# Layer 1 of a two-layer AdaLN model: extra work beside the attention tiles placed anew, and part of VectorE's work given to GpSimd

## The chip, the core and the metric

The kernel runs on one core of a Trainium2 chip, in one launch. The metric is the device time in microseconds. TensorE multiplies matrices and transposes, VectorE and ScalarE read and write both SBUF and PSUM, GpSimd works on SBUF alone and issues the indirect DMAs, and SyncE issues nearly all other DMAs. Each engine runs its own instructions strictly in the order in which they are written, and they wait for one another on semaphores. So an instruction that waits holds up everything behind it on its engine.

## The reference

Eight sequences of 512 tokens with 128 channels go through two layers; each adds a gated attention branch and then a gated feed-forward branch to `x`:

```python
h = _layernorm(x) * (1 + ca) + sa
x = x + ga * attention(h)
h = _layernorm(x) * (1 + cb) + sb
x = x + gb * feed_forward(h)
```

In layer 0 the attention is a Nystrom one with an iterated inverse, and the feed-forward is a top-1 mixture of experts with a capacity. In layer 1 the attention has 16 heads of 8 channels, a bias that depends on the distance of query and key, and a gate, `a * sigmoid(g)`. Its feed-forward is a whole block of its own:

```python
x = x + _mla(_rmsnorm(x, g1), Wq, Wdkv, Wuk, Wuv, Wo)      # 16 causal heads
x = x + _moe(_rmsnorm(x, g2), gate_w, w1, w2)              # top 2 of 8 experts
```

## The kernel before

**Two phases.** Layer 0 takes the first 650 us or so and is not touched. Layer 1 (`layer1_phase`) is one software pipeline of 713 steps. Two attentions run through it, tile by tile. A tile is 128 queries of one head against up to 512 keys; a batch (one sequence) has 64 tiles, so each attention has 512 tiles. Attention `a=0`, the one with the bias, takes tile `m` in step `m`. Attention `a=1`, the causal one, follows `LATE = 136` steps later. So steps 0 to 135 hold one attention, 136 to 511 both (the mixed steps), and 512 to 647 the second alone. I call 64 steps a block: block `s` is steps `64s` to `64s+63`, and `i` is the step within it.

**What one step does.** For `a=0`: TensorE forms the scores, VectorE adds the bias strip and takes the row maximum (`shift`, L2601, into `l_XY`), GpSimd forms maximum minus score (`L2053`), TensorE transposes the tile three steps after the shift (L2350), ScalarE takes the exponential out of PSUM (L2162), and TensorE multiplies by the values for four tiles at a time (L2384). For `a=1`: scores, VectorE's masked maximum, a second score product in turned form (L2361, with the maxima as three more rows of `l_stack`), the exponential, the values. TensorE may run at most three score tiles ahead of VectorE's shifts, since `ps` banks 0 to 2 hold them.

**The extras.** Everything else is written into these steps by hand, by tables of step numbers:

- `pre(b)`: the layer-0 experts' output is gathered (`gather`, L2042, four indirect DMAs), scaled (L2662), added to `x` (L2668), normalised and projected to q, k, v of `a=0`.
- `mid(b)`: the gate of attention 0 is applied (L2689, L2694), `x` updated (L2698), then a layer norm (L2632, L2710, L2713), an RMS norm and the projections for `a=1`.
- `split`: q and k are each cut into three bf16 parts. VectorE subtracts the first part (L2652) and casts the second (L2655); GpSimd forms the third (`last_part`, L2103). `store_parts` writes the parts to DRAM, and `stack_up` reads them back into `l_stack`, six DMAs for 16 tiles.
- `router(b)`: top-2 routing of batch `b`, from step `MOE_START[b]` on (44 of a block, for nearly all). `scatter` (L2077) sends tokens to DRAM with eight indirect DMAs, and `plan_blocks` (L2814 to L2861) makes, once for two batches, the table of expert blocks. Then come the block pairs of experts (L2484, L2459) and the gathers that combine them (L2092).

**What is where, before.** In a mixed block, VectorE's extras stand at i = 3, 7, 9, 11 (`pre`), 22 to 28 (splits of `a=0`), 23 to 43 (`mid`), and 49 to 55 (splits of `a=1`). The plan is at 30, 32, 34, 36 and 38 in blocks 5 and 7. GpSimd's scatters are at 18 to 32, one in two steps, and the gathers at 40, 44, 48 and 52. SyncE stores the parts of `a=1` at 57, waits there until they have landed, and loads the first stack of the next batch at 62. `CLEAR_AT` has it zero 2 MB of `rows_dram` at i = 56 of blocks 0, 2, 3, 4 and at step 130.

## Time and profile before

| | |
|---|---|
| median of 3 runs | 1846.85 us (1842.99 to 1851.0) |
| the profiled execution | 1861.73 us, its span 1860.0 us |
| mean granted TensorE clock | 0.95 |
| busy: TensorE | 1617.7 us (87%) |
| busy: VectorE | 1326.5 us (71%) |
| busy: ScalarE | 1007.1 us (54%) |
| busy: GpSimd | 779.3 us (42%) |

The profiled execution took 0.8% more than the median of the runs. Its shares of busy time are means over stages with different limits, so they do not say what bounds a stage. TensorE's matmuls are pipelined and their ends are modelled: a TensorE shown as 100% busy need not be at its peak, but idle time shown there is idle. Windows below are in us from the span's start. Step 0 of layer 1 starts at about 693 us (the first shift on VectorE), step 136 at 849 us, step 512 at about 1571 us, and the last tile of `a=1` is shifted at 1816 us.

### The profile page before, as it was taken

To read this page: it belongs to the slowest core of one execution; us is meant where nothing else is said; L and a number is where in the kernel's file an instruction comes from. 1 tells how busy PE (TensorE), PEld (TensorE's weight loads), DVE (VectorE), ACT (ScalarE), POOL (GpSimd) and SP (SyncE) were. 2 spreads that over 40 slices of the span, in tenths; PEclk is the share of its full clock that TensorE was granted. 3 is DMA by queue.
4 is the path that set the end of the run, shared out by engine and by line. 5 is a ranking of instruction groups with operands and counts; after the bars stand their busy time and mean duration, and the time that the engine had idled before them with its cause. 6 is when DMAs were issued, how large, how long until landed. Compare 5 with 4: busy or idle time off the path is not lost.

```text
span 1860.0 us, 50554 instructions
## 1 busy us (share of the span) xinstructions
PE 1617.7 (87%) x19264; PEld 1179.7 (63%) x19264; DVE 1326.5 (71%) x4176; ACT 1007.1 (54%) x2196; POOL 779.3 (42%) x1021
## 2 busy tenths in 40 slices
PE   3899898899883939989999999989999988888887
PEld 2677676777772727766666666656767766544545
DVE  6678777876761127788778798897886786685646
ACT  1545454455451316665666667666666656564532
POOL 3111311220115237786656566565464574243210
PEclk7899999999995969999999999999999999988999
DMA  3631122122004424344423325143452333535321
GB/s 111 190 94 46 40 84 65 36 69 82 5 7 122 157 81 155 131 151 151 160 64 128 125 84 164 56 147 98 131 161 88 114 127 111 161 98 162 109 62 53
DMA packets 143839, 194.53 MB, mean 105 GB/s; under 512 B 21920, under 2 KB 110176, under 8 KB 142320
## 3 DMA queue, kind: packets, MB, share of 16 engines
q1 hardware_dynamic: 129312, 171.75, 29.6%
q0 software_dynamic: 5760, 14.03, 2.4%
q10 hardware_dynamic: 8528, 5.51, 1.0%
q8 instruction: 156, 2.56, 0.6%
q14 instruction: 83, 0.68, 0.1%
HBM read 142.39 MB, written 50.69 MB: 104 GB/s over the span
## 4 chain that ended last, share of the span: by engine, by line
PE 44%; DVE 9%; issue 7%; ACT 5%; DMA 1%; POOL 1%; SPq 0%; another core or an unknown queue 0%; ACTq 0%; POOLq 0%; DVEq 0%
PE ps L2350 9%; PE ps L2333 7%; PE ps L2384 6%; PE ps L2394 3%; DVE l_XY L2601 3%; PE ps L2361 3%; ACT PT L2162 2%; PE ps L1229 2%; PE ps L2484 2%; PE ps L1238 2%; PE ps L2459 2%; PE ps L2410 2%; DVE ps L2601 1%; PE ps L2431 1%; PE ps L2522 1%
## 5 line engine op out<-in xcount | busy, mean ns | idle before, releaser
L2053 POOL TENSOR_SCALAR l_XY<-l_XY,l_nmax 128x512 f32<-128x512 f32 x512 | 374.9, 737 | 295.9 <-DVE l_nmax L2601 287.6
L2601 DVE CUSTOM_DVE_ANT_0 l_XY<-ps,strips 128x512 f32<-128x512 f32 x512 | 347.7, 687 | 170.4 <-PE ps L2333 115.2
L2162 ACT ACTIVATE PT<-ps 128x512 f32<-128x512 f32 x512 | 307.3, 601 | 248.0 <-PE ps L2350 236.3
L2333 PE MATMUL ps<-l_stack 72*128 72x512 bf16 (+3 forms) x1024 | 350.9, 348 | 50.1 <-DVE l_nmax L2601 35.5
L2350 PE MATMUL ps<-ident,l_XY 128*128 128x128 f32 x2048 | 320.6, 279 | 1.7 <-ACT PT L2162 1.4
L2350 PEld LDWEIGHTS ps<-ident,l_XY 128*128 128x128 f32 x2048 | 236.9, 142 | 91.0 <-issue 56.8
L2601 DVE CUSTOM_DVE_ANT_0 ps<-ps,mask 128x384 f32<-128x384 f32 (+3 forms) x512 | 250.2, 496 | 24.3 <-PE ps L2333 20.2
L2361 PE MATMUL ps<-l_stack 75*128 75x256 bf16 (+3 forms) x512 | 157.2, 308 | 22.0 <-ACT PT_odd L2165 7.5
L2333 PEld LDWEIGHTS ps<-l_stack 72*128 72x128 bf16 x1024 | 101.1, 99 | 100.5 <-DVE l_nmax L2601 55.7
L2384 PE MATMUL ps<-PT,v_aug 128*10 128x128 f32 x4096 | 137.6, 275 | 6.8 <-ACT l_O_sb L2171 6.4
L2165 ACT ACTIVATE PT_even<-ps 128x512 f32<-128x512 f32 (+1 forms) x256 | 125.1, 494 | 22.8 <-PE ps L2363 17.3
L2384 PEld LDWEIGHTS ps<-PT,v_aug 128*10 128x10 f32 x4096 | 100.3, 92 | 39.1 <-ACT PT L2162 12.4
L531 POOL DMA_INDIRECT slots_in<-h,slot_all x32 | 32.5, 1016 | 207.6 <-DVE slot_all L1106 200.3
L2363 PE MATMUL ps<-mask_turned,ident_b 128*128 128x128 bf16 x512 | 113.9, 223 | 0.0
L2601 DVE DVE_READ_ACCUMULATOR2_ANT l_nmax<- 128x1 f32 x1024 | 113.3, 111 | 0.0
L2165 ACT ACTIVATE PT_odd<-ps 128x384 f32<-128x384 f32 (+1 forms) x256 | 98.4, 388 | 27.4 <-PE ps L2363 15.0
L684 PE MATMUL ps<-X,AV 64*64 64x64 f32 x2560 | 92.7, 221 | 13.4 <-DVE X L1125 12.7
L684 PEld LDWEIGHTS ps<-X,AV 64*64 64x64 f32 x2560 | 81.8, 134 | 27.0 <-DVE X L1125 12.6
L684 PE MATMUL ps<-AV,Q 64*64 64x128 f32 (+1 forms) x1280 | 78.0, 275 | 23.5 <-DVE Q L1125 23.5
L2361 PEld LDWEIGHTS ps<-l_stack 75*128 75x128 bf16 x512 | 51.0, 100 | 66.1 <-issue 18.4
L684 PEld LDWEIGHTS ps<-AV,Q 64*64 64x64 f32 x1280 | 68.8, 141 | 30.3 <-DVE Q L1125 27.0
L2363 PEld LDWEIGHTS ps<-mask_turned,ident_b 128*128 128x128 bf16 x512 | 50.9, 99 | 46.9 <-issue 5.3
(372 smaller groups left out, 3215.9 us busy)
## 6 DMA issues: line engine op xcount, KB each, us to landing
l_stack<-parts_dram SPq DMA_DIRECT2D x384, 96.0 KB
...
rows_dram<-mask SPq DMA_DIRECT2D x6, 2048.0 KB, 8.9
...
```

Of the source, the lines that this page charges most:

```text
L684: last = nc.tensor.matmul(out(h), lhs(h), rhs(h), start=True, stop=True)
L1229: nc.tensor.matmul(ps[:, 2 + f, :], w1_e[:, e, f * P:(f + 1) * P], xT_e[:, e % 2], start=True, stop=True).then_inc(hidden_ready, 1)
L2053: nc.gpsimd.tensor_scalar(XY[:, c % XY_BUFS], XY[:, c % XY_BUFS], -1.0, nmax[:, c % 8:c % 8 + 1], ALU.mult, ALU.add).then_inc(y_pool, 1)
L2162: nc.scalar.activation(PT[:, u % QUADS, j], src.rearrange("p (k q) -> p k q", q=P), ACT.Exp).then_inc(moved, 1)
L2165: nc.scalar.activation(turned_keys(q)[:, j], src[:, 0:T - q * P], ACT.Exp).then_inc(moved, 1)
L2333: nc.tensor.matmul(ps[:, n % 3, 0:w], stack[0:STACK, 0, h, q * P:(q + 1) * P], stack[0:STACK, 1, h, 0:w], start=True, stop=True).then_inc( ...
L2350: last = nc.tensor.transpose(ps[:, to, k * P:(k + 1) * P], XY[:, c % XY_BUFS, k * P:(k + 1) * P], ident[:])
L2361: nc.tensor.matmul(ps[:, to, 0:T - k * P], stack[:, 1, h, k * P:(k + 1) * P], stack[:, 0, h, k * P:T], start=True, stop=False)
L2363: nc.tensor.matmul(ps[:, to, 0:P], ident_b[:], mask_turned[:], start=False, stop=True).then_inc(turned, 1)
L2384: last = nc.tensor.matmul(o[32 * j:32 * j + VW], v[:, k, 4 * head_group(0, g) + j, :], PT[:, u % QUADS, j, k, :], start=(k == 0), stop=(k ...
L2394: last = nc.tensor.matmul(ps[32 * j:32 * j + VW, o_bank(1, g), k * P:T], v_aug[1][u // 16 % 2][:, k, 4 * (g % 4) + j, :], turned_keys(k)[: ...
L2601: nc.vector.tensor_tensor_reduce(out=dst, in0=src, in1=add, scale=-1.0, scalar=3.0e38, op0=ALU.add, op1=ALU.min, accum_out=low).then_inc(s ...
```

## The change

No matrix product is added or taken away. `s` and `i` are as above.

- **split**: for all but the first batch, VectorE writes the second bf16 part straight from the subtraction, one instruction in place of two. GpSimd does the subtraction into `qk` once more (`first_less`) before `last_part`.
- **additions to x** in `pre` and `mid` go from VectorE to GpSimd (`x_added`, `x_gated`).
- **the layer norm of `mid`**: four `tensor_scalar` and two wide tensor instructions become eight `scalar_tensor_tensor` of 128 columns.
- **places**: tables `MID`, `LAST_MID`, `PRE` name the steps. The scaling of the gathered rows goes from i = 3 of a block to i = 53 and 62 of the block before. The gathers stand at 44, 47, 49, 50. The plan is in six pieces at i = 27, 29, 37, 41, 43, 46. Scatters go one in four steps, i = 17 to 45. Other extras move by a few steps.
- **SyncE**: the wait for the landed parts goes from the store to the load that needs them. The parts of `a=0` are stored at 44 and not at 30, those of `a=1` at 62 and not at 57. The first stack of a batch of `a=1` is loaded at 65 (i = 1) and not at 62; for the last batch, step 577 and not 570.

```diff
-MIXED_STAGES = dict(wo=1, add=3, square=5, ..., count=28, place=37, gates=37, scatter=38, plan=(50, 52, 54, 56, 58), fold=41)
+MIXED_STAGES = dict(wo=3, add=5, square=9, ..., count=26, place=36, gates=36, scatter=37, plan=(47, 49, 57, 61, 63, 66), fold=41)
...
-SCATTER_EVERY = {0: 2, 1: 2, 2: 2, 3: 2, 4: 4, 5: 1}
+SCATTER_EVERY = {0: 4, 1: 4, 2: 4, 3: 4, 4: 3, 5: 1}
...
-GATHER_AT = 40
+PRE_GATHERS, MID_GATES = (44, 47, 49, 50), (19, 20)
...
-    steps += [(LATE + GROUP * k - 10 - (4 if k >= 27 else 0), 1, k) for k in range(4 * B)]
+    steps += [(LATE + GROUP * k - (7 if k % 4 == 0 else 10 + (4 if k >= 27 else 0)), 1, k) for k in range(4 * B)]
...
-                    sp.wait_ge(parts_stored, 32 * n + 32)
 
                 def stack_up(a, k):
                     b = k // 4
+                    if k % 4 == 0:
+                        sp.wait_ge(parts_stored, 32 * PART_NO[a, b] + 32)
...
-                    if pre is not None and i == 30:
+                    if pre is not None and i == PRE["store"]:
                         store_parts(0, pre)
-                    if mid is not None and i == 57:
+                    if mid is not None and i == mid_of(mid)["store"]:
                         store_parts(1, mid)
...
+                def x_added(b):
+                    pool.wait_ge(y_scaled, E + b)
+                    nc.gpsimd.tensor_tensor(x_rows(b), x_rows(b), y0[:], ALU.add).then_inc(x_in, 1)
+
+                def x_gated(b):
+                    pool.wait_ge(mid_sum, E + b + 1)
+                    nc.gpsimd.tensor_tensor(x_rows(b), x_rows(b), h_of(b), ALU.add).then_inc(x_mid, 1)
+
+                def first_less(k, a, b):
+                    pool.wait_ge(second_part, 2 * PART_NO[a, b] + k + 1)
+                    order.link(nc.gpsimd.tensor_tensor(qk[:, k, :], qk[:, k, :], parts[:, k, 0, :], ALU.subtract))
...
-                        link(nc.vector.tensor_tensor(qk[:, k, :], qk[:, k, :], parts[:, k, 0, :], ALU.subtract))
+                        if PART_NO[a, b]:
+                            nc.vector.tensor_tensor(parts[:, k, 1, :], qk[:, k, :], parts[:, k, 0, :], ALU.subtract).then_inc(second_part, 1)
...
-                def pre(b, i):
-                    if i == 3:
+                def scaled(b, half_):
+                    if half_ == 0:
                         dve.wait_ge(gathered, 16 * TT * (b + 1))
...
+                    if m == pre_step(b, "y0"):
+                        scaled(b, 0)
+                    if m == pre_step(b, "y1"):
+                        scaled(b, 1).then_inc(y_scaled, 1)
...
-                    if i == 33:
-                        wait_xn(("xm", b))
-                        link(normalised(1, b))
+                    if i == mid_of(b)["norm"]:
+                        dve.wait_ge(var_ready, VARIANCES[1, b] + 1)
+                        for t in range(TT):
+                            last = nc.vector.scalar_tensor_tensor(out=h[:, t, :], in0=x_tile(b, t), scalar=mean_var[1][:, t, 0:1],
+                                                                  in1=mid_rows[:, 2], op0=ALU.subtract, op1=ALU.mult)
+                        link(last)
```

VectorE in steps 356 and 357 (block 5, i = 36 and 37), before. L2713 is the second wide instruction of the layer norm, L2842 to L2849 a piece of the plan; the shifts (`ISA`) are the tiles' own work.

```order
L2710 TENSOR_TENSOR h_tok<-l_xn,mid_rows 128x512 [waits l1_dve_order]
L2601 ISA l_XY,l_nmax<-ps,strips 128x512 [waits scores_ready,turned]
L2601 ISA l_nmax 128x1
L2601 ISA ps,l_nmax<-ps,mask 128x512 [waits scores_ready]
L2601 ISA l_nmax 128x1
L2842 TENSOR_REDUCE block_at<-l_gated 128x24 [waits l1_dve_order]
L2845 TENSOR_SCALAR plan<-expert_of 128x24
L2847 TENSOR_TENSOR block_at<-block_at,block_row 128x24 [waits l1_dve_order]
L2849 TENSOR_SCALAR plan<-block_at 128x24 [waits l1_dve_order]
L2601 ISA l_XY,l_nmax<-ps,strips 128x512 [waits scores_ready,turned]
L2601 ISA l_nmax 128x1
L2601 ISA ps,l_nmax<-ps,mask 128x512 [waits scores_ready]
```

The same two steps in the changed kernel:

```order
L2645 ISA l_nmax 128x1
L2645 ISA ps,l_nmax<-ps,mask 128x512 [waits scores_ready]
L2645 ISA l_nmax 128x1
L2645 ISA l_XY,l_nmax<-ps,strips 128x512 [waits scores_ready,turned]
L2645 ISA l_nmax 128x1
L2645 ISA ps,l_nmax<-ps,mask 128x512 [waits scores_ready]
L2645 ISA l_nmax 128x1
L2774 SCALAR_TENSOR_TENSOR h_tok<-h_tok,l_rstd,mid_rows 128x128 [waits l1_rstd_ready,l1_dve_order]
L2774 SCALAR_TENSOR_TENSOR h_tok<-h_tok,l_rstd,mid_rows 128x128 x3
L2890 SCALAR_TENSOR_TENSOR shift_of<-first_row,start_of 128x8 [waits l1_dve_order]
L2892 TENSOR_TENSOR l_gated<-block_row,start_of 128x192
L2895 TENSOR_TENSOR l_gated<-l_gated,named 128x192 [waits l1_dve_order]
```

The four instructions of the plan have left step 356, and in step 357 the narrow norm instructions stand together with an earlier piece of the plan.

SyncE where block 1 ends and block 2 begins, before. `parts_dram<-l_parts` stores the parts of the first batch of `a=1`; `x6` is its first stack, and the two rows behind it are a stack of `a=0`.

```order
L1869 DMA parts_dram<-l_parts 128x3x512 [waits l1_parts_ready] x2
L1836 DMA gb_now<-mods_dram 128x128 [waits l1_x_in,l1_parts_stored]
L1836 DMA mid_rows<-mods_dram 128x128 [waits mid_rows_used]
L1836 DMA mid_rows<-mods_dram 128x128 x2
L1883 DMA l_stack<-parts_dram 24x1x2048 x6
L1883 DMA l_stack<-parts_dram 24x1x2048 [waits scores_ready]
L1883 DMA l_stack<-parts_dram 24x1x2048 x5
```

In the changed kernel:

```order
L1855 DMA mid_rows<-mods_dram 128x128 [waits mid_rows_used]
L1855 DMA mid_rows<-mods_dram 128x128 x2
L1888 DMA parts_dram<-l_parts 128x3x512 [waits l1_parts_ready] x2
L1903 DMA l_stack<-parts_dram 24x1x2048 [waits scores_ready]
L1903 DMA l_stack<-parts_dram 24x1x2048 x5
L1903 DMA l_stack<-parts_dram 24x1x2048 [waits l1_parts_stored]
L1903 DMA l_stack<-parts_dram 24x1x2048 x5
```

The store now stands behind the rows of `mid`, the stack of `a=0` comes ahead of that of `a=1`, and the wait for the landed parts is at the latter.

SyncE shortly before tile 448 of `a=1` (its last batch), before. `l_stack<-max_rows` brings the maxima that the turned scores of an earlier stack need.

```order
L1869 DMA parts_dram<-l_parts 128x3x512 [waits l1_stacked3,l1_stacked2,l1_stacked4,l1_parts_ready]
L1869 DMA parts_dram<-l_parts 128x3x512 [waits l1_parts_ready]
L1883 DMA l_stack<-parts_dram 24x1x2048 [waits scores_ready,l1_parts_stored]
L1883 DMA l_stack<-parts_dram 24x1x2048 x5
L1915 DMA l_stack<-max_rows 3x16x128 [waits moved]
```

In the changed kernel:

```order
L1888 DMA parts_dram<-l_parts 128x3x512 [waits l1_stacked3,l1_stacked2,l1_stacked4,l1_parts_ready]
L1888 DMA parts_dram<-l_parts 128x3x512 [waits l1_parts_ready]
L1935 DMA l_stack<-max_rows 3x16x128 [waits moved]
L1903 DMA l_stack<-parts_dram 24x1x2048 [waits scores_ready,l1_parts_stored]
L1903 DMA l_stack<-parts_dram 24x1x2048 x5
```

The maxima now go ahead of the six loads of the stack, and not behind them.

## Rows read from the trace of the kernel before

**Rows 1.** Busy time by windows, steps 22 to 40 of blocks 1 to 7

```profile
1218.00:1256.00 38.00, 30.50 (x333) 21.23 (x331) 36.68 (x118) 22.92 (x56) 24.15 (x33) 1.00 0.36 118
...
1484.00:1518.00 34.00, 29.06 (x317) 20.04 (x315) 32.63 (x113) 20.37 (x52) 25.17 (x33) 0.95 0.33 111
sum 223.00, PE 198.37 PEld 140.86 DVE 211.76 ACT 141.08 POOL 150.54; mean PE 28.34 PEld 20.12 DVE 30.25 ACT 20.15 POOL 21.51
```

**Rows 2.** The same view, steps 0 to 14 of blocks 1 to 6

```profile
sum 136.00, PE 126.21 PEld 92.46 DVE 123.10 ACT 81.01 POOL 71.97; mean PE 21.03 PEld 15.41 DVE 20.52 ACT 13.50 POOL 11.99
```

**Rows 3.** The same view, steps 48 to 62 of blocks 1 to 6

```profile
sum 161.00, PE 157.44 PEld 106.34 DVE 116.58 ACT 109.75 POOL 96.13; mean PE 26.24 PEld 17.72 DVE 19.43 ACT 18.29 POOL 16.02
```

**Rows 4.** Waits, TensorE, 693 to 1571 us: total us, times, longest

```profile
PE ps L2333 <- DVE l_nmax L2601: 31.9, 52, 1.4
```

**Rows 5.** Lines of VectorE: count, busy us, mean ns, idle us before

```profile
L2632 DVE TENSOR_SCALAR l_xn<-x_sb,l_mean_var,l_rstd 128x128 f32<-128x128 f32 x60 | 23.8, 457 | 0.2 <-POOL l_rstd L2048 0.2
...
L2655 DVE CAST l_parts<-l_qk 128x512 bf16<-128x512 f32 x30 | 17.3, 578 | 0.0
...
L2662 DVE SCALAR_TENSOR_TENSOR y<-y,gate_keep,gb_now 128x128 f32<-128x128 f32 x28 | 9.6, 401 | 1.4 <-DMA gb_now<-mods_dram 1.4
...
L2698 DVE TENSOR_TENSOR x_sb<-x_sb,h_tok 128x512 f32<-128x512 f32 x8 | 7.2, 903 | 0.0
L2710 DVE TENSOR_TENSOR h_tok<-l_xn,mid_rows 128x512 f32<-128x512 f32 x8 | 7.1, 882 | 0.0
...
L2713 DVE TENSOR_TENSOR h_tok<-h_tok,mid_rows 128x512 f32<-128x512 f32 x8 | 6.3, 783 | 0.0
```

**Rows 6.** The same view, first and last of eleven in the plan

```profile
L2834 DVE TENSOR_REDUCE expert_of<-l_gated 128x24 f32<-128x192 f32 x3 | 1.0, 345 | 0.0
...
L2861 DVE CAST placed_index<-placed 128x16 int32<-128x16 f32 x3 | 0.5, 174 | 0.1
```

**Rows 7.** The same view, GpSimd

```profile
L2103 POOL TENSOR_TENSOR l_parts<-l_qk,l_parts 128x512 bf16<-128x512 f32 x30 | 34.9, 1164 | 2.4 <-DVE l_parts L2655 2.2
...
L2099 POOL TENSOR_TENSOR l_gated<-l_gated,b_gate_sb 128x512 f32<-128x512 f32 x16 | 20.7, 1293 | 9.9 <-ACT l_gated L2193 9.8
```

**Rows 8.** One line's instructions, L2698: durations in ns

```profile
L2698 DVE TENSOR_TENSOR x_sb<-x_sb,h_tok x8: 681/700/1515, 795.9 to 1621.8; 128x512 f32<-128x512 f32 x8
```

**Rows 9.** Timeline of VectorE and GpSimd in block 5: start, length

```profile
1225.25 2.15 DVE L2694 SCALAR_TENSOR_TENSOR h_tok<-h_tok,mid_rows 128x512 f32<-128x512 f32 x1
...
1225.68 1.16 POOL L2103 TENSOR_TENSOR l_parts<-l_qk,l_parts 128x512 bf16<-128x512 f32 x1
```

**Rows 10.** Timelines of the gathers' end and of SyncE; the page's DMA issues

```profile
664.05 1.01 POOL L2042 DMA_INDIRECT y<-slots_out,slot_all  x1 [0.30 <-issue]
...
666.67 1.14 DVE L2662 SCALAR_TENSOR_TENSOR y<-y,gate_keep,gb_now 128x128 f32<-128x128 f32 x4 [8.74 <-DMA y<-slots_out,slot_all]
...
748.76 0.58 SPq L1959 DMA_DIRECT2D rows_dram<-mask  x1
...
rows_dram<-mask SPq DMA_DIRECT2D x6, 2048.0 KB, 8.9
```

**Rows 11.** Timelines of SyncE and TensorE, end of block 1

```profile
829.61 5.29 SPq L1869 DMA_DIRECT2D parts_dram<-l_parts  x2
837.47 0.33 SPq L1836 DMA_DIRECT2D gb_now<-mods_dram  x1
...
839.27 8.36 SPq L1883 DMA_DIRECT2D l_stack<-parts_dram  x12
...
848.12 0.22 PE L2333 MATMUL ps<-l_stack 72*128 72x128 bf16 x1
```

**Rows 12.** Timelines of SyncE and TensorE, 1655 to 1665 us

```profile
1657.60 4.16 SPq L1883 DMA_DIRECT2D l_stack<-parts_dram  x6
1661.80 0.78 SPq L1915 DMA_DIRECT2D l_stack<-max_rows  x1
...
1664.50 0.59 PE L2361 MATMUL ps<-l_stack 75*128 75x512 bf16 x1 [2.34 <-DMA l_stack<-max_rows]
```

More of the change, by code:

```diff
@@ L2110, in _ @@
                 for m in range(STEPS):
+                    for b in range(1, B):
+                        if m == pre_step(b, "x"):
+                            x_added(b)
                     s, i = divmod(m, TILES)
@@ new lines, in first_pre @@
+                def first_pre():
+                    scaled(0, 0)
+                    link(scaled(0, 1))
+                    linked()
+                    nc.vector.tensor_tensor(x_rows(0), x_rows(0), y0[:], ALU.add).then_inc(x_in, 1)
+                    dve.wait_ge(x_in, 1)
+                    statistics(0, 0)
+                    linked()
+                    variance(0)
+                    normalised(0, 0).then_inc(tok_ready, 1)
+                    for k in range(2):
+                        for part in range(2):
+                            split(k, 0, 0, part)
@@ L2886, in router @@
                         gate_pair(b)
-                    if b == GROUPS[g][-1] and k in p["plan"]:
-                        plan_blocks(g, p["plan"].index(k))
+                    for step in range(len(p["plan"])):
+                        if b == GROUPS[g][-1] and k == p["plan"][step]:
+                            plan_blocks(g, step)
                 def block_product(n):
```

157 lines of the change are left out of this document (86 added, 71 removed).

## The prediction

> **What bounds the kernel now.** I read the busy times by window first. Up to 693 us nothing changes, so only the 1167 us behind that count. In the seven stretches of steps 22 to 40, one in each of blocks 1 to 7, VectorE is busy for 211.8 of 223 us (95%) and TensorE for 198.4, so TensorE is idle for 24.6 us [rows 1]. The two worst are those with the plan, blocks 5 and 7: idle 38.0 - 30.5 = 7.5 us and 34.0 - 29.1 = 4.9 us. In steps 0 to 14 of six blocks VectorE has 123.1 of 136 us (91%) and TensorE is idle for 9.8 us [rows 2]. In steps 48 to 62 it is the other way round: TensorE 157.4 of 161 us (98%), VectorE 116.6 (72%) [rows 3]. The waits name the cause: TensorE's scores waited 31.9 us in 52 places for VectorE to free a bank of scores [rows 4]. So VectorE bounds two stretches of each block and TensorE the rest. A microsecond taken from VectorE counts in the first two only, and only up to TensorE's idle time there.
>
> **VectorE relieved, steps 22 to 40.** For each block with both parts of the work: two casts go, 2 x 0.578 = 1.16 us; the addition to `x` goes, 0.90 us; the norm goes from 4 x 0.457 + 0.882 + 0.783 = 3.49 us to eight narrow instructions, which the trace has in one form like them at 0.401 us, 3.21 us, so 0.28 us goes [rows 5]. That is 2.3 us. Of the plan, eleven instructions leave the stretch; the first takes 0.345 us and the last 0.174 us [rows 6], at a mean between them of 0.26 us some 2.9 us. So block 5 sheds 5.2 us against 7.5 us idle; block 7, which has no casts there, sheds 0.90 + 0.28 + 2.9 = 4.1 us against 4.9 us; the other five shed 2.3 x 5 = 11.7 us against 24.6 - 12.4 = 12.2 us. Sum 21.0 us.
>
> **Steps 0 to 14.** Four scalings (4 x 0.401 us [rows 5]) and an addition of the form of L2698 (0.90 us) leave, 2.5 us in each of six blocks, 15 us, against 9.8 us idle [rows 2]: 9.8 us at most. The scalings reappear at i = 53 and 62, where VectorE has 28% to spare; that hides them [rows 3], and without that cover they would cost 1.6 us a block.
>
> **How much of the 30.8 us comes.** At most all of it, at least nothing. VectorE's remaining work is in lumps of up to eight small instructions in a step, and TensorE's lead is three score tiles. In steps 0 to 14, where VectorE is busy for 91%, TensorE still idles for 7% of the time [rows 2]; seven points of 223 us in the other stretches would be 15 us of idle that stays. I take half, **-15.5 us**.
>
> **GpSimd.** It gets two subtractions per split pair and an addition, which I price by the two-input rows at 1.16 and 1.29 us [rows 7]; two of its eight scatters leave steps 22 to 40. It was busy 150.5 of 223 us there [rows 1]: 67%. Added 2 x 1.16 + 1.29 = 3.6 us less about 2 x 1 us is 1.6 us in 32, so 72%. It negates a tile two steps before TensorE needs it, which hides lumps of up to some 3 us. At nothing, up to 3 us in block 0 where steps are short.
> What it does to VectorE is another matter. The addition L2698 took 0.68 us at least, 0.70 in the median and 1.52 at most [rows 8], and the scaling at 1225.25 us took 2.15 us while GpSimd formed a third part [rows 9]. So VectorE's work on two SBUF operands stretches beside GpSimd's. The half above contains this at about 4 us.
> The Trainium skill (GPSIMD Engine Reference, Key points) says that GpSimd shares its SBUF interfaces with VectorE and contends with VectorE instructions that have two SBUF inputs. By that rule the trace agrees. It speaks against the change, since work taken from VectorE for GpSimd comes back as longer VectorE instructions; a rival below takes it to its end.
>
> **The gather's landing, new in VectorE's queue.** The scaling of the gathered rows now stands at i = 53, three steps behind the last gather (i = 50), with VectorE's shifts queued behind it and TensorE, GpSimd and ScalarE behind those. The last of the first gathers was issued at 664.05 us and VectorE went on at 666.67 us [rows 10]: 2.6 us, on quiet queues. In block 0 a step takes about 1 us, and SyncE zeroes 2 MB from 748.76 us on, which takes 8.9 us to land [rows 10], just where the last gather would be issued (749 to 750 us). VectorE comes to the scaling at about 751 us. If the gather lands behind the zeroes, at 757 us, it waits 6 us, less about 3 us that TensorE has in hand; if it lands in 2.6 us, about 1 us. Bounds 0 and 6, I take **+3 us**. In later blocks three steps are 4.5 to 6 us: nothing, at most 2 us each.
>
> **The first stack of `a=1`, moved behind a stack of `a=0`.** Before, SyncE issued the parts by 834.9 us, had them landed at 837.47, and issued both stacks from 839.27 on, 4.2 us each; TensorE took the first score of `a=1` at 848.12 us [rows 11]. Now GpSimd makes the last part three steps later and in two instructions, about 839 us; SyncE issues the stack of `a=0` until 843.3 and that of `a=1` until 847.5 us, and the landing comes after. It took 2.6 us for the parts (834.9 to 837.47), so 850 us at the earliest and 854 us if two stacks at once slow it. The wait is 2 to 6 us, **+3.5 us**. TensorE's queue stands, and all others with it. In later blocks a step takes 1.5 to 2 us, the load is needed six steps on (9 us or more) and takes 4.2 + 4.2 us of issuing plus the landing, from a store that is itself three steps earlier than step 65: nothing, at most 2 us each.
>
> **Late: the maxima ahead of the stack.** At 1657.60 us SyncE issues six loads for 4.2 us, and the maxima behind them at 1661.80; TensorE waits 2.34 us for them [rows 12]. In the new order they go first. The wait of 2.3 us goes; what is late next is the stack, issued until about 1662.5 us and needed near 1668. Some more may come back, since TensorE's next products run slowly behind that wait. Bounds 0 and 6, **-3 us**. The other tables of the last 290 us move work by a step or two among engines that are not full; at nothing, between -4 and +4 us.
>
> **Sum.** -15.5 + 3 + 3.5 - 3 = -12 us. Against the profiled execution (1861.7 us) that is 1849.7; the median of the runs is 14.9 us lower, so 1846.85 - 12 = **1835 us**. By the skill's rule, taken to its end, the first term is nothing and the sum +3.5 us.
>
> **The rivals.**
> *Given back through the shared memory.* GpSimd's 30 more subtractions and 15 additions are 30 x 1.16 + 15 x 1.29 = 54 us of two-input work, and each of VectorE's remaining two-input instructions that meets one is stretched by up to its length, as at 1225.25 us (+1.5 us). If 15 to 20 of them are met, all that VectorE sheds is gone. For it: rows 8 and 9. Against it: GpSimd is idle for a third of the time, and the median of L2698 is hardly stretched. About 1850 us, within 0.5%.
> *The gather holds VectorE in every block* (the slower side). The zeroing stands at the same place in blocks 0, 2, 3 and 4, and the gathers are now packed into seven steps. If each landing waits for 2 MB of zeroes, block 0 costs 6 us and the others 3 to 4 us each, some 16 us, with the stack's full 6 us 22; less a relief of 10, +12 us: 1859 us. It decides from the point where the last gather takes more than about 5 us to land in a mixed block. For it: the 8.9 us of row 10. Against it: three mixed steps are 5 to 6 us, and the gather is issued a little ahead of the zeroes.
> *Nearly all of VectorE's share comes.* 25 of 30.8 us, 6 us late, the stalls small: 1846.85 - 27 = 1820 us. It speaks for it that the stretches with the most idle time are the ones relieved most; against it that VectorE stays the fullest engine there.
>
> **How the numbers follow.** Half a per cent is 9 us, about what a measurement of this kernel can tell from no change. The forecast (relief of about half, two small stalls; 1828 to 1843 us) has 0.42, of it 0.34 below 1837.6 us and 0.08 above. Nearly all comes: 0.12, faster. Given back: 0.24, of it 0.22 the same and 0.02 slower. The gather in every block: 0.22, of it 0.20 slower and 0.02 the same. So faster 0.46, same 0.32, slower 0.22. The range must take in most of each neighbour: 1819 to 1858 us; the forecast alone would be 1828 to 1843.
>
> **What would show it.** The casts fall from 30 to none behind the first batch, and the subtraction stays near 0.8 us. In steps 22 to 40 TensorE's idle falls from 24.6 us to about 14, with the most in blocks 5 and 7, and its waits for `l_nmax` from 31.9 to under 20 us. VectorE waits for a DMA into `y` near 751 us for 2 to 6 us. TensorE waits for a DMA into `l_stack` once, near 850 us, for 2 to 6 us. The wait for the maxima near 1662 us is gone. I am wrong if VectorE's two-input rows are longer than before by 0.2 us or more in the mean, if the waits for `y` stand in every block, or if TensorE's idle in steps 22 to 40 does not fall.

## The result

| | before | changed |
|---|---|---|
| median of 4 runs, us | 1846.09 (1842.99 to 1851.0) | 1823.99 (1820.67 to 1834.29) |
| ratio, 95% interval | | 0.988 (0.9847 to 0.9913) |
| span of the profiled execution, us | 1860.0 | 1825.2 |

The change takes 22.1 us off (16 to 28 by the interval), and the forecast was 12 (1835 us). The span fell by more, 34.8 us, because the two profiled executions also differ where the change hardly does anything: step 0 starts 5.1 us earlier. A finer measure is needed. In this text a step starts where VectorE's shift of its newest score tile starts in the trace (L2601 before, L2645 now; a tile of `a=0` up to step 511, of `a=1` from 512 on). By it:

| us | before | changed |
|---|---|---|
| start of step 0 | 693.1 | 688.0 |
| blocks 0 to 3 | 68.6, 79.1, 101.8, 115.4 | 75.2, 79.2, 102.5, 110.7 |
| blocks 4 to 7 | 118.7, 128.3, 135.6, 131.8 | 111.8, 117.8, 134.4, 128.0 |
| steps 0 to 512 | 879.4 | 859.6 |
| step 512 to the end | 287.5 | 277.6 |

The eight blocks give 19.8 us, nearly all of the measured gain. Blocks 0 and 2 are longer than before, blocks 3, 4, 5 and 7 shorter; blocks 1 and 6 differ by less than they vary between runs (see below).

**After, by windows.** Busy time of each engine in steps 22 to 40 of blocks 1 to 7 (blocks 5 and 7, and the sum), to be read against [rows 1]; then steps 0 to 14 of blocks 1 to 6 (block 2 and the sum) and steps 48 to 62, against [rows 2, 3].

```profile
1207.00:1239.00 32.00, 29.84 (x331) 21.11 (x329) 30.43 (x106) 21.50 (x48) 24.92 (x31) 1.00 0.33 108
...
1464.00:1494.00 30.00, 28.68 (x327) 20.52 (x326) 29.29 (x104) 20.04 (x46) 22.94 (x30) 1.00 0.36 119
sum 207.00, PE 196.58 PEld 142.09 DVE 192.19 ACT 140.47 POOL 159.59; mean PE 28.08 PEld 20.30 DVE 27.46 ACT 20.07 POOL 22.80
```

```profile
842.00:863.00 21.00, 17.50 (x216) 12.37 (x214) 14.64 (x58) 9.88 (x18) 13.44 (x19) 0.92 0.58 189
...
sum 134.00, PE 128.28 PEld 93.52 DVE 112.39 ACT 80.95 POOL 77.84; mean PE 21.38 PEld 15.59 DVE 18.73 ACT 13.49 POOL 12.97
```

```profile
sum 163.00, PE 160.17 PEld 108.04 DVE 115.35 ACT 111.59 POOL 108.56; mean PE 26.70 PEld 18.01 DVE 19.22 ACT 18.60 POOL 18.09
```

In steps 22 to 40 the sum went from 223 to 207 us, VectorE from 211.8 to 192.2 us busy, and TensorE's idle time from 24.6 to 207.0 - 196.6 = 10.4 us. In block 5 the window is 32 us long instead of 38. In steps 0 to 14 VectorE went from 123.1 to 112.4 us, but the sum only from 136 to 134, since block 2 alone has TensorE idle for 21.0 - 17.5 = 3.5 us. That is one of the two new stalls. Steps 48 to 62 stay TensorE's, 160.2 of 163 us.

**TensorE's waits, steps 0 to 512**: total us, times, longest.

```profile
PE ps L2377 <- DVE l_nmax L2645: 14.7, 24, 3.9
PE ps L2394 <- POOL l_XY L2073: 3.7, 4, 1.1
...
PE ps L2377 <- DMA l_stack<-parts_dram: 2.3, 1, 2.3
```

The wait for VectorE's maxima fell from 31.9 us in 52 places [rows 4] to 14.7 in 24, and 3.9 us of what is left stand in one place, the first stall:

```profile
743.88 0.59 SPq L1979 DMA_DIRECT2D rows_dram<-mask  x1
...
745.26 1.05 POOL L2062 DMA_INDIRECT y<-slots_out,slot_all  x1 [0.17 <-issue]
...
751.74 0.61 DVE L2708 SCALAR_TENSOR_TENSOR y<-y,gate_keep,gb_now 128x128 f32<-128x128 f32 x2 [5.13 <-DMA y<-slots_out,slot_all]
```

These are rows of the timelines of SyncE, GpSimd and VectorE. The zeroing was issued at 743.88 us, the last gather at 745.26, and VectorE, at the scaling, stood 5.13 us until it landed. From the last gather's issue to its use it is 6.5 us, against 2.6 us on quiet queues [rows 10]. The second stall, on the timelines of SyncE and TensorE, answers to [rows 11]:

```profile
836.39 4.07 SPq L1888 DMA_DIRECT2D parts_dram<-l_parts  x2
840.51 8.36 SPq L1903 DMA_DIRECT2D l_stack<-parts_dram  x12
...
852.41 0.29 PE L2377 MATMUL ps<-l_stack 72*128 72x128 bf16 x1 [2.33 <-DMA l_stack<-parts_dram]
```

The stack of `a=0` goes out first, that of `a=1` until 848.87 us, and TensorE waits 2.33 us until 852.41.

**Lines of VectorE, then of GpSimd**: count, busy us, mean ns, idle us before.

```profile
L2696 DVE TENSOR_TENSOR l_parts<-l_qk,l_parts 128x512 bf16<-128x512 f32 x30 | 21.5, 716 | 0.2 <-ACT l_parts L2249 0.2
...
L2774 DVE SCALAR_TENSOR_TENSOR h_tok<-h_tok,l_rstd,mid_rows 128x128 f32<-128x128 f32 x32 | 13.5, 479 | 0.0
...
L2767 DVE SCALAR_TENSOR_TENSOR h_tok<-x_sb,l_mean_var,mid_rows 128x128 f32<-128x128 f32 x32 | 12.7, 457 | 0.0
L2708 DVE SCALAR_TENSOR_TENSOR y<-y,gate_keep,gb_now 128x128 f32<-128x128 f32 x28 | 10.9, 431 | 8.6 <-DMA y<-slots_out,slot_all 7.9 <-DMA gb_now<-mods_dram 0.7
...
L2756 DVE SCALAR_TENSOR_TENSOR h_tok<-h_tok,mid_rows 128x512 f32<-128x512 f32 x8 | 6.0, 748 | 0.0
```

```profile
L2131 POOL TENSOR_TENSOR l_qk<-l_qk,l_parts 128x512 f32<-128x512 f32 x30 | 35.7, 1189 | 19.4 <-DVE l_parts L2696 19.4
L2136 POOL TENSOR_TENSOR l_parts<-l_qk,l_parts 128x512 bf16<-128x512 f32 x30 | 35.4, 1181 | 0.7
...
L2127 POOL TENSOR_TENSOR x_sb<-x_sb,h_tok 128x512 f32<-128x512 f32 x8 | 10.1, 1267 | 4.8 <-DVE h_tok L2756 4.8
...
L2123 POOL TENSOR_TENSOR x_sb<-x_sb,y 128x512 f32<-128x512 f32 x7 | 9.0, 1281 | 8.1 <-DVE y L2708 8.1
```

The casts of 0.578 us [rows 5] are gone behind the first batch. GpSimd's two-input rows cost what they cost before [rows 7].

**Late**, SyncE and TensorE, against [rows 12]:

```profile
1631.24 0.76 SPq L1935 DMA_DIRECT2D l_stack<-max_rows  x1
1632.10 8.40 SPq L1903 DMA_DIRECT2D l_stack<-parts_dram  x12
...
1639.64 0.23 PE L2377 MATMUL ps<-l_stack 72*128 72x128 bf16 x1 [0.77 <-DMA l_stack<-parts_dram]
...
1650.98 0.38 PE L2377 MATMUL ps<-l_stack 72*128 72x384 bf16 x1 [3.91 <-DVE l_nmax L2645]
```

The maxima now leave ahead of the stack. Steps later TensorE waits 3.91 us in one go for VectorE, a gap that the kernel before doesn't have there.

### The profile page after: what moved, and what is told of

Read it like the earlier page. It is cut to its first block, busy times and chain, and to the rows that moved or that the text cites. A ratio compares the mean times of both kernels' runs of the same rounds, so it can differ in the third digit from the quotient of the medians.

```text
span 1825.2 us, 50593 instructions
## 1 busy us (share of the span) xinstructions
PE 1610.8 (88%) x19264; PEld 1175.9 (64%) x19264; DVE 1296.3 (71%) x4147; ACT 1006.3 (55%) x2196; POOL 818.1 (45%) x1066
## 4 chain that ended last, share of the span: by engine, by line
PE 44%; DVE 6%; issue 6%; ACT 4%; POOL 4%; DMA 3%; SPq 1%; POOLq 0%; ACTq 0%; DVEq 0%
PE ps L2394 10%; PE ps L2377 7%; PE ps L2428 6%; PE ps L2438 3%; PE ps L2405 3%; DVE l_XY L2645 2%; PE ps L2528 2%; PE ps L1230 2%; PE ps L2503 2%; PE ps L1239 2%; ACT PT L2204 1%; PE ps L2454 1%; POOL l_XY L2073 1%; PE ps L2475 1%; SPq L1903 1%
## 5 line engine op out<-in xcount | busy, mean ns | idle before, releaser
L2645 DVE CUSTOM_DVE_ANT_0 l_XY<-ps,strips 128x512 f32<-128x512 f32 x512 | 348.5, 687 | 170.0 <-PE ps L2377 123.1
L2073 POOL TENSOR_SCALAR l_XY<-l_XY,l_nmax 128x512 f32<-128x512 f32 x512 | 365.0, 719 | 217.3 <-DVE l_nmax L2645 211.4
L2645 DVE CUSTOM_DVE_ANT_0 ps<-ps,mask 128x384 f32<-128x384 f32 (+3 forms) x512 | 250.7, 497 | 18.9 <-PE ps L2377 18.9
L2645 DVE DVE_READ_ACCUMULATOR2_ANT l_nmax<- 128x1 f32 x1024 | 113.8, 111 | 0.0
L2207 ACT ACTIVATE PT_odd<-ps 128x384 f32<-128x384 f32 (+1 forms) x256 | 98.1, 388 | 24.6 <-PE ps L2407 20.6
L684 PE MATMUL ps<-AV,Q 64*64 64x128 f32 (+1 forms) x1280 | 74.3, 267 | 23.6 <-DVE Q L1125 23.6
L684 PEld LDWEIGHTS ps<-AV,Q 64*64 64x64 f32 x1280 | 65.1, 136 | 30.4 <-DVE Q L1125 27.0
```

The source lines that it names most:

```text
L684: last = nc.tensor.matmul(out(h), lhs(h), rhs(h), start=True, stop=True)
L2073: nc.gpsimd.tensor_scalar(XY[:, c % XY_BUFS], XY[:, c % XY_BUFS], -1.0, nmax[:, c % 8:c % 8 + 1], ALU.mult, ALU.add).then_inc(y_pool, 1)
L2207: nc.scalar.activation(turned_keys(q)[:, j], src[:, 0:T - q * P], ACT.Exp).then_inc(moved, 1)
L2645: nc.vector.tensor_tensor_reduce(out=dst, in0=src, in1=add, scale=-1.0, scalar=3.0e38, op0=ALU.add, op1=ALU.min, accum_out=low).then_inc(s ...
```

## The experiments

All are edits of the changed kernel. They ran in three groups on three chips, each group with the kernel before beside it (medians 1863 to 1867 us there, against 1846 in the result), so only their ratios to before are compared with 0.988. The changed kernel was not run again in these groups, and the kernel before has no other profile than that of the result, so in the first two rows the ratio and the times of steps are the result's own.

| edit of the changed kernel | ratio, 95% interval | steps 0 to 512, us | steps 22 to 40, blocks 1 to 7, us |
|---|---|---|---|
| before | 1 | 879.4 | 222.6 |
| changed | 0.988 (0.9847 to 0.9913) | 859.6 | 205.4 |
| e1 scaling behind landing | 0.9874 (0.9854 to 0.9894) | 856.6 | 206.1 |
| e9 zeroing later | 0.9885 (0.9863 to 0.9907) | 856.5 | 206.2 |
| e2 stack first | 0.987 (0.9851 to 0.9888) | 857.8 | 206.1 |
| c1 e9 and e2 | 0.9858 (0.9831 to 0.9885) | 850.9 | 205.7 |
| c2 c1, one addition back | 0.9891 (0.9867 to 0.9914) | 857.1 | 206.1 |
| e11 casts back | 0.9909 (0.9876 to 0.9942) | 862.1 | 208.1 |
| e4 casts and additions back | 0.9949 (0.993 to 0.9968) | 872.7 | 212.8 |
| e6 plan back | 0.9951 (0.9933 to 0.9969) | 869.4 | 215.6 |
| e10 placement back | 1.0066 (1.0043 to 1.0088) | 891.1 | 232.2 |
| e12 e10, scatters apart | 1.0092 (1.0062 to 1.0121) | 896.4 | 224.7 |
| e7 late part back | 0.9907 (0.9889 to 0.9925) | 859.8 | 206.4 |
| c3 c1, late plan spread | 0.99 (0.9881 to 0.9919) | 852.7 | 206.1 |

How far the third column can be trusted: blocks 3, 4 and 5 took 110.7, 111.8 and 117.8 us in the changed kernel and, on another chip, 110.7, 112.0 and 118.1 us in e9, and as much within 0.1 us in e1, e2 and c1. Blocks 1, 2, 6 and 7 vary by up to 3 us where nothing was edited. The ratios are a second witness for the distance to before: times 1846 us they make +12 us for e10, -9 for e4 and -26 for c1, where the steps give +11.7, -6.7 and -28.5.

**e1: the scaling behind the landing.** Block 0 alone, where the stall is:

```diff
-    if b == 1:
+    if b in (1, 2):
         at = dict(PRE, y0=3, y1=5, x=7, statistics=9, var=11, power=12, xn=13)
-        return at[stage]
+        return TILES * (b - 1) + at[stage]
```

> The changed kernel with one edit: batch 2's scaling of the gathered rows (and what follows on it up to the norm) stands again at i = 3 to 13 of the step group behind, as for batch 1, and no longer at i = 53, where VectorE waited 5.1 us for the gather at 746.6 to 751.7 us. My theory: that wait was paid in full, so steps 48 to 56 of block 0 fall from 13.3 to about 8 us, TensorE's idle time there goes, and about 1.5 us comes back in the next steps as VectorE's load: -3 to -5 us against the changed kernel, some 1820 us. The rival (TensorE had enough in hand, or another wait stands right behind): less than 1.5 us, and steps 48 to 56 stay above 11 us.

Block 0 fell from 75.2 to 70.0 us, steps 48 to 56 from 13.3 to 9.0. Block 1 was 1.1 us longer (80.3), within its spread. The stall was paid, at 4 to 5 us; the rival falls.

**e9: the zeroing later.**

```diff
-CLEAR_AT = (56, 130, 184, 248, 312)
+CLEAR_AT = (66, 130, 184, 248, 312)
```

> The changed kernel with one number: the second of the 2 MB zeroings is issued at step 66 instead of 56, so it no longer starts (743.9 us) ahead of the last gather (745.3 us). This tells what made the gather late. My theory of the prediction: the zeroes did, and without them the gather lands about 2.6 us behind its issue, so VectorE's wait falls from 5.1 us to 1.5 to 2.5 us. The rival: three gathers in seven steps, or the stack load beside them, are late by themselves; then the wait stays at 4.5 us or more. The time: -2 to -3 us under the first, 0 under the second.

The last gather and the scaling, timelines of GpSimd and VectorE:

```profile
748.95 1.05 POOL L2062 DMA_INDIRECT y<-slots_out,slot_all  x1 [0.17 <-issue]
...
751.62 1.30 DVE L2708 SCALAR_TENSOR_TENSOR y<-y,gate_keep,gb_now 128x128 f32<-128x128 f32 x2 [1.34 <-DMA y<-slots_out,slot_all]
```

The wait fell from 5.13 to 1.34 us, and from the gather's issue to the scaling it is 2.7 us instead of 6.5. So the zeroes held the gather up, as the prediction argued from [rows 10]. Block 0: 70.7 us, 4.5 less.

**e2: the stack of `a=1` first.**

```diff
-(7 if k % 4 == 0 else 10 + (4 if k >= 27 else 0))
+(8 if k % 4 == 0 and k < 28 else 7 if k % 4 == 0 else 10 + (4 if k >= 27 else 0))
```

> The changed kernel with one number: the first stack of each batch of a=1 is loaded one step earlier (step offset -8 instead of -7, k < 28), which puts it ahead of the stack of a=0 on SyncE instead of behind. My theory: TensorE's wait near 852 us is the time that SyncE issues the other stack (4.2 us), so the wait falls from 2.3 us (and steps 8 to 16 of block 2 from 14.8 us) to near nothing and about 12 us: -2 to -3 us. The rival: the parts are late (SyncE waits for their landing in any order), so that the a=1 stack is no earlier and the a=0 stack is late too: the wait stays within 0.5 us, the time the same or up to 1 us longer.

TensorE's waits around the place:

```profile
PE ps L2377 <- DVE l_nmax L2645: 1.1, 2, 0.9
PE ps L2394 <- POOL l_XY L2073: 0.7, 1, 0.7
```

No wait for the stack is left, and steps 8 to 16 of block 2 took 11.1 us, against 14.8 in the changed kernel and 14.3 and 14.5 in e9 and e1. The loss was the order of two loads on SyncE. Its size varies: with the late order kept, e4 and e7 took 12.9 and 12.6 us there, so the stall cost from 1.5 to 3.7 us.

**e4 and e11: the division of the work.** e11 puts the cast back on VectorE (GpSimd loses its second subtraction), e4 both additions to `x` too. The core of e4, abbreviated:

```diff
-    nc.vector.tensor_tensor(parts[:, k, 1, :], qk[:, k, :], parts[:, k, 0, :], ALU.subtract)
+    nc.vector.tensor_tensor(qk[:, k, :], qk[:, k, :], parts[:, k, 0, :], ALU.subtract)
+    # two steps on: nc.vector.tensor_copy(parts[:, k, 1, :], qk[:, k, :])
-    x_added(b)   # GpSimd
-    x_gated(mid) # GpSimd
+    nc.vector.tensor_tensor(x_rows(b), x_rows(b), y0[:], ALU.add)
+    nc.vector.tensor_tensor(x_rows(b), x_rows(b), h, ALU.add)
```

> The changed kernel with its placements, but with the work divided as in the kernel before: the cast of each split and both additions to x on VectorE again (the norm stays in its new form). My theory: the relief of VectorE is what brought the 30 us of the mixed blocks, and placement little, so most of it goes: windows 22 to 40 of blocks 1 to 7 from about 205 us back to about 218, steps 0 to 14 from 133 to about 136, in all +13 to +20 us, 1838 to 1846 us. The rival (the placements brought it: plan in six pieces, scaling moved, scatters one in four): at most +6 us, about 1828 us.

> The changed kernel with only the cast of each split on VectorE again, two steps behind its subtraction (no second subtraction on GpSimd); the additions to x stay on GpSimd. 15 pairs of casts of 0.58 us are 17 us of work. Theory: each microsecond on VectorE in steps 22 to 40 is one of time, outside them none. The pre split (i = 24 to 29) lies inside, the mid split (i = 51 to 55) outside, so half of it, 7 x 1.16 = 8 us: steps 0 to 512 some 866 us, and windows 22 to 40 some 213 us as with the whole division put back (212.8). The rival (the adds are what counted): 860 to 862 us.

e4 cost 13.1 us in steps 0 to 512, the lower end of what was expected, and 0.0069 in the ratio. But placement keeps 6.7 us with both stalls in it, so "placement little" was wrong. The 13.1 us do not lie where the theory had them: steps 22 to 40 rose by 7.4 us and steps 48 to 64, where VectorE has room, by 11.1 (5.0 of it in block 1, which varies by 2.4 by itself), while steps 0 to 14 fell by 5.8. e11 cost 2.5 us, where 6 to 8 were expected, and steps 22 to 40 rose by 2.7 and not by 7 to 8: a cast pair there is mostly hidden, and its rival (the additions count, 860 to 862 us) came closer with 862.1. So the additions make the larger share of e4's 13.1 us.

**e10 and e12: the placement.** e10 keeps the new division and puts the mixed steps' tables back (MID, PRE, MIXED_STAGES, scatters, gathers, expert pairs, the stack's place). GpSimd's first subtractions had no place before; in e10 each stands one step ahead of its third part. e12 changes one number of e10:

```diff
-SCATTER_EVERY = {0: 2, 1: 2, 2: 2, 3: 2, 4: 3, 5: 1}
+SCATTER_EVERY = {0: 4, 1: 4, 2: 4, 3: 4, 4: 3, 5: 1}
```

> The changed kernel with its division of the work (no casts, both additions to x on GpSimd, norm in the new form, plan in six parts), but with the mixed steps' placements of the kernel before: tables MID and PRE, MIXED_STAGES (plan at 50, 50, 52, 54, 56, 58), scatters one in two, gathers at 40, 44, 48, 52, the stack of a=1 in its old place. The late tables stay as changed. With the kernel before, the changed one and the one whose division was put back (872.7 us for steps 0 to 512, against 859.6 changed and 879.4 before) this is the fourth corner of a square. If division and placement simply add (division 13 us, placement 6.7 us, in which two stalls of some 9 us are contained), steps 0 to 512 take 879.4 - 13.1 = 866 us. My theory now is that the placements without their two stalls are worth as much as the division, and that the two need each other: 866 to 872 us, the stalls gone. The rival (the division alone brings all, the placements only their stalls): 850 to 856 us.

> The kernel with the mixed steps' placements put back (steps 0 to 512: 891.1 us, against 879.4 before), with one number more: scatters one step in four again, as changed, instead of one in two. There TensorE had gaps of 2.5 us at step 31 of block 4 and step 30 of block 5 for a tile that GpSimd had still to negate, and ran at half clock behind each. My theory: GpSimd was the bound there, with scatters, a first subtraction and a third part one step apart, so spreading the scatters takes both gaps away: steps 22 to 40 of blocks 1 to 7 from 232 to 218 us or less, steps 0 to 512 to about 875 us. The rival (the places of the splits or VectorE's plan decide, the scatters not): no less than 886 us.

Both expectations for e10 failed: 891.1 us, 11.7 more than before. The new division in the old places is slower than the kernel before, at least with GpSimd's new instructions where e10 has them. GpSimd and then TensorE in block 4, and TensorE's granted clock around it:

```profile
1115.50 1.15 POOL L2129 TENSOR_TENSOR l_qk<-l_qk,l_parts 128x512 f32<-128x512 f32 x1
1117.44 1.03 POOL L2095 DMA_INDIRECT rows_dram<-l_xf,row_index  x1 [0.79 <-POOL l_qk L2129]
1118.51 0.70 POOL L2071 TENSOR_SCALAR l_XY<-l_XY,l_nmax 128x512 f32<-128x512 f32 x1
...
1119.36 0.63 PE L2392 MATMUL ps<-ident,l_XY 128*128 128x128 f32 x4 [2.46 <-POOL l_XY L2071]
```

```profile
1100.00:1138.00 38.00, 32.95 (x330) 22.47 (x328) 28.87 (x98) 21.57 (x52) 27.20 (x35) 0.91 0.37 123
1117.00:1122.00 5.00, 2.15 (x12) 1.63 (x13) 2.73 (x13) 1.51 (x3) 4.35 (x5) 0.89 0.20 66
1122.00:1127.00 5.00, 5.00 (x51) 2.88 (x49) 2.31 (x8) 1.35 (x3) 4.69 (x7) 0.50 0.55 168
```

The first subtraction and a scatter stand in a row on GpSimd, the tile's negation behind them, and TensorE waits 2.46 us for that tile. Then its clock is granted at 0.50 (the 1.2 GHz level) from 1122 to 1127 us, where it is fully busy and does less; over the whole window TensorE is busy for 32.95 us, against 29.14 in the changed kernel's 1095 to 1125. Steps 22 to 40 of this block took 37.5 us, 4.3 more than before.

With the scatters apart (e12) steps 22 to 40 of block 4 fell from 37.5 to 32.2 us: GpSimd's row was the bound there. All the same steps 0 to 512 rose to 896.4, because a stall of another kind came up in block 5 (5.3 us) and block 7 (7.0 us). Waits of TensorE, then SyncE's timeline and its wait:

```profile
PE ps L2403 <- DMA l_stack<-max_rows: 5.3, 1, 5.3
```

```profile
1256.79 1.21 SPq L1968 DMA_DIRECT2D w_own<-table_dram  x2
1271.34 1.20 SPq L1953 DMA_DIRECT2D x_b<-rows_dram  x2
1272.58 0.84 SPq L1933 DMA_DIRECT2D l_stack<-max_rows  x1
```

```profile
SPq L1948 <- DMA rows_dram<-l_xf,row_index: 12.8, 1, 12.8
```

These rows are of block 5. SyncE stood for 12.8 us for the last scatter, which now comes later, to load the first rows of the expert pairs. The maxima for TensorE were queued behind it and left at 1272.58. The changed kernel has its expert pairs eight and three steps later, the counterpart of its scatters. That the scatters alone bring nothing is shown; that the later pairs would mend e12 was not run.

**e6: the plan back.**

```diff
-plan=(47, 49, 57, 61, 63, 66)
+plan=(50, 50, 52, 54, 56, 58)
```

> The changed kernel with the plan in its old places: the six pieces at 50, 50, 52, 54, 56, 58 instead of 47, 49, 57, 61, 63, 66, which puts eleven instructions more of VectorE into steps 22 to 40 of blocks 5 and 7. My prediction priced them at 2.9 us in each. Theory: they count there in full: block 5 steps 22 to 40 from 31.6 to about 34.5 us, block 7 from 30.1 to about 33 us, all else the same within 1 us: +5 to +6 us. The rival (VectorE has room for them since the casts and the addition are gone): +2 us or less in both together.

Steps 22 to 40 of block 5 took 37.6 us instead of 31.6, of block 7 34.0 instead of 29.8 (30.1 to 30.5 in the other runs): 9.8 in steps 0 to 512, more than the 5.8 us priced for the instructions moved. Block 5 in e6 (the window and four us of it), TensorE's waits there, and the same steps in c1:

```profile
1216.00:1254.00 38.00, 31.52 (x331) 21.82 (x329) 35.58 (x117) 21.94 (x48) 25.68 (x32) 0.96 0.28 94
1244.00:1248.00 4.00, 4.00 (x47) 2.64 (x49) 3.93 (x11) 1.56 (x3) 2.82 (x4) 0.60 0.66 226
```

```profile
PE ps L2377 <- DVE l_nmax L2645: 5.8, 5, 1.9
```

```profile
1206.00:1238.00 32.00, 30.05 (x330) 20.78 (x329) 30.74 (x106) 21.29 (x49) 25.32 (x32) 1.00 0.33 110
```

VectorE has 35.6 of 38 us; TensorE waits 5.8 us for it, and after 1.9 us of that in one piece its clock is at 0.60 for four us. But most of the excess over the price is VectorE's own. The eleven instructions took 5.5 us here, not 2.9, because three of them were stretched, each beside a wide two-input instruction of GpSimd. The two worst, and what ran beside them (timelines of VectorE and GpSimd):

```profile
1241.08 1.35 DVE L2900 TENSOR_TENSOR l_gated<-l_gated,expert_of 128x192 f32<-128x192 f32 x1
1245.31 1.16 DVE L2909 TENSOR_SCALAR plan<-expert_of 128x24 int32<-128x24 f32 x1
```

```profile
1241.06 1.16 POOL L2136 TENSOR_TENSOR l_parts<-l_qk,l_parts 128x512 bf16<-128x512 f32 x1
1245.28 1.16 POOL L2131 TENSOR_TENSOR l_qk<-l_qk,l_parts 128x512 f32<-128x512 f32 x1
```

In block 7 of e6, where no split stands, the same two took 0.36 and 0.17 us and all eleven 3.0. TensorE's gap of 1.9 us ends at 1243.49, behind the shift that follows the first of the two. So 5.5 us of instructions cost 6.0 us in block 5 and 3.0 us cost 3.5 to 4.2 in block 7: they count in full, as expected, and what comes on top, the lower clock included, is 0.5 to 1.2 us.

**e7: the late part back.** LATE_STAGES, DENSE_STAGES, LAST_STAGES and COMBINE as before, and the stack of k = 28 ahead of the maxima.

> The changed kernel with the late part as before: tables for the late and dense blocks, the combines, and the stack of k = 28 behind which the maxima wait. Steps 0 to 512 are untouched (within 1.5 us of 859.6). From step 512 to the end the kernel before took 287.5 us, the changed one 277.6 in its profile, but 286.1 to 292.8 us in the profiles of its variants on the other chip. Prediction: the new late part is worth 3 us (TensorE's wait of 2.3 us for the maxima), so this run takes some 3 us longer than the variants, about 292 us, and TensorE's wait for the maxima near step 588 is back at 2 to 3 us. The rival (what is saved there is lost to the clock or to the plan in one lump, a gap of 3.9 us that only the changed kernels have): no difference, 286 to 290 us.

```profile
PE ps L2408 <- DMA l_stack<-max_rows: 4.5, 2, 3.9
```

Waits of TensorE from 1650 us: the wait for the maxima is back, 3.9 us at the longest, and yet step 512 to the end took 289.9 us, inside the 285.7 to 292.9 of the ten variants that have the changed late part. So the 9.9 us that this part fell between the first two profiles is mostly not the change's. The ratio's interval overlaps that of 0.988. What the late part is worth isn't settled; nothing here shows a gain.

**c1, c2, c3: the repairs.** c1 has the edits of e9 and e2. c2 adds to c1 the addition behind the scaling on VectorE again. c3 adds to c1:

```diff
-LATE_STAGES: plan=(32, 32, 33, 34, 35, 36)
+             plan=(33, 34, 35, 36, 37, 38)
-PAIR_WINDOWS: (1, MOE_START[3] + 71, 12, 4)
+              (1, MOE_START[3] + 73, 12, 4)
```

> The changed kernel with the two repairs that each did its part alone: second zeroing at step 66, first stack of a=1 one step earlier. Steps 0 to 512 took 859.6 us changed, 856.5 and 857.8 us with one repair each. If the two add up: 855 us or a little under, VectorE's wait for the gathered rows near 1.3 us and steps 8 to 16 of block 2 near 11.1 us; -5 us against the changed kernel, a ratio to before near 0.985. The rival (one stall, repaired, shows another, as the zeroing at 66 lies nearer to the stack loads): no less than 857 us.

> The two repairs, and one addition to x (that behind the scaling of the gathered rows, once a batch at i = 63) on VectorE again, the gated one stays on GpSimd. With the whole division put back, steps 0 to 15 of blocks 1 to 6 took 133.6 us against 139.2 changed; 3 of those us are the stack's stall. Theory: at i = 63 VectorE has room and GpSimd is held up by its scatters, and VectorE's statistics wait for the sum, so the addition is done sooner on VectorE: -2 to -3 us against the kernel with the repairs alone, in steps 0 to 15. The rival (GpSimd's share was no bound, VectorE's 0.9 us in each of six blocks counts): up to +3 us.

> The kernel with the two repairs (steps 0 to 512: 850.9 us, ratio to before 0.986) and two more numbers: the last plan's pieces at 33, 34, 35, 36, 37, 38 instead of 32, 32, 33, 34, 35, 36, against the gap of 3.9 us in which TensorE waits for VectorE at step 588; and the second window of expert pairs two steps later, against TensorE's wait of 0.4 to 1.8 us for rows of x at step 425. Theory: the gap falls below 2.5 us and with it the half clock behind it: -1 to -3 us, a ratio near 0.984. The rival (the lump is the top choice and placing around it, not the plan; the plan two steps later delays the last pairs): the gap stays within 0.5 us or the pairs' wait takes its place, 0 to +2 us.

c1: steps 0 to 512 in 850.9 us, 8.7 under the changed kernel, of it 4.8 in block 0 and 3.6 in block 2. Its ratio, 0.9858, is the best of all; in whole runs the two intervals overlap, so that it beats the changed kernel is shown for these blocks only.
c2: steps 0 to 8 fell by 0.7 to 0.8 us in blocks 1, 2, 4 and 5, but steps 56 to 64 of blocks 2, 3 and 4 rose by 1.3 each: VectorE takes the addition in its place there. Steps 0 to 512 took 857.1 us, 6.2 more than c1 (2.9 of it in steps 40 to 48 of block 6, which vary by 1.9 unedited). No gain; the rival holds in its sign, and the time is above its +3 us.
c3: the gap stayed, and a new one came up where expert pairs wait for their weights:

```profile
PE ps L2377 <- DVE l_nmax L2645: 6.2, 6, 3.8
...
PE ps L2528 <- DMA w_own<-table_dram: 2.2, 1, 2.2
```

The longest wait for `l_nmax` is 3.8 us, so spreading the plan does not take the gap away. VectorE's timeline has the same thing there in the changed kernel and in c3: four instructions that combine the experts' output (L2964 to L2975, 3.2 us in a row), right behind one piece of the plan (0.9 and 1.1 us). Moving the combine was not tried. Steps 512 to 576 rose from 89.6 to 94.3 us.

## Why the prediction was right

The sign, the mechanism and the two stalls were right. The step that failed in size is the first term of the sum, the half taken of TensorE's idle time. The measured 1824.0 us lies outside the forecast's own 1828 to 1843 us and nearer to the rival "Nearly all of VectorE's share comes" (1820 us, chance 0.12); it is in the stated range, 1819 to 1858 us, because that takes in most of the neighbours.

| term | predicted | measured, steps 0 to 512 |
|---|---|---|
| VectorE relieved, in steps 22 to 40 and 0 to 14 | -15.5, between 0 and -30.8 | -24.4 (-16.9 and -7.5, c1 against before) |
| all other steps, beside the stalls | 0 | -4.1 (c1: -28.5 in all) |
| gather's landing, block 0 | +3 (0 to 6) | +4.5 to +5.2 (block 0 in e9 and e1) |
| stack of `a=1` | +3.5 (2 to 6) | +3.2 to +3.7 (steps 8 to 16 of block 2, e2 and c1 against e1, e9, changed); +1.5 to +1.8 against e7 and e4 |
| maxima ahead of the stack, other late tables | -3 | not settled, none seen (e7) |
| sum | -12 | -22.1 median; -19.8 in steps 0 to 512 |

**The relief.** I took half of TensorE's idle time because "VectorE's remaining work is in lumps". Against c1, which has neither stall, steps 22 to 40 give 16.9 of the 21.0 us priced and steps 0 to 14 7.5 of the 9.8: four fifths and not half. I had reckoned with 15 us of idle time that stays; in steps 22 to 40 of the changed kernel it is 10.4 us. Two more things were wrong. First, I priced the placements at nothing beside the plan and the stalls. e10 shows that the division, in the old places, costs 11.7 us, and with the new placement it is worth 13.1 us (e4): the two can't be added. Steps 40 to 48 of blocks 1 to 7, on which the prediction has no word, went from 101.8 to 89.6 us (c1) and stay at 104.6 in e10, so this is the placement's; part of it is TensorE's work that now stands elsewhere (95 us busy there before, 87 in c1), and the remaining steps are 8.1 us longer. Which table brings the net 4.1 us was not run. Second, "counts in the first two only" is not so: in e4 more was lost in steps 48 to 64 than in steps 22 to 40. That the sum came out 10 us off and no more is partly luck: the relief was too small by 9 us, the unpriced steps gave 4, the stalls cost 1 to 2 us more than priced, and of the 3 us late nothing was seen.

**Single terms inside it.** The plan I priced at 5.8 us for two blocks; e6 gives 9.8, mostly since in block 5 it collides with GpSimd's subtractions. The norm I had at -0.28 us a block, with rows of 0.401 us; the eight new ones took 0.457 and 0.479, so 3.7 us against 3.49, a little longer than before. GpSimd "at nothing" held only because its work was spread: TensorE waited 3.7 us in four places for it.

**The rival of the shared memory** fell as a price, and not as a mechanism. The Trainium skill (GPSIMD Engine Reference, Key points) says that GpSimd contends with VectorE instructions that have two SBUF inputs. The trace agrees, row by row. Two such instructions, before and changed (one line's instructions: shortest, median, longest in ns):

```profile
L2694 DVE SCALAR_TENSOR_TENSOR h_tok<-h_tok,mid_rows x8: 678/1292/2351, 792.3 to 1619.1; 128x512 f32<-128x512 f32 x8
L2756 DVE SCALAR_TENSOR_TENSOR h_tok<-h_tok,mid_rows x8: 676/680/1220, 793.1 to 1593.2; 128x512 f32<-128x512 f32 x8
```

```profile
L2737 DVE TENSOR_TENSOR l_xf<-h_tok,l_rstd x8: 673/692/694, 1051.6 to 1818.1; 128x512 f32<-128x512 f32 x8
L2800 DVE TENSOR_TENSOR l_xf<-h_tok,l_rstd x8: 683/696/1565, 1048.7 to 1784.3; 128x512 f32<-128x512 f32 x8
```

The first took 1.328 us in the mean before, when four of the eight met a wide two-input instruction of GpSimd (1.84 us each), and 0.748 now, when none does. The second went from 0.689 to 0.895: now four of the eight meet one (1.10 us each). By the prediction's own sign of being wrong (0.2 us or more in the mean) this one line speaks for the rival. The subtraction of a split took 0.716 us in the mean against 0.823, but it now writes bf16. The sum decides. An estimate from the records of steps 0 to 512: what VectorE's instructions without a PSUM operand took beyond the shortest of their form is 55 us before and 46 us in the changed kernel, although GpSimd's wide two-input work there went from 51 to 102 us. So the added work did not come back as longer rows, because the new places keep most of it apart; where e6 puts the plan beside it, it does.

**The rival of the gather in every block** fell too: VectorE waited for `y` twice in all 28 scalings, 5.1 us and 2.8 us. Its mechanism (zeroes ahead of the gather) is the one that e9 shows, in block 0 alone, where a step takes about a microsecond.

**The stalls** came as priced from the order on the queues. The stack's times were forecast as 843.3, 847.5 and 850 us or later; they were 844.7 (half of the 8.36 us from 840.51), 848.87 and 852.41.

**Late**: the predicted wait is gone, and a wait of 3.9 us that the prediction does not have stands a few steps off, behind the combine and a piece of the plan in one lump on VectorE.
